# A product-based recommender on one core: fields of the last two batch tiles handled one by one, GpSimd given fewer pairs, and three matmul groups held back

## What is computed

```python
embed = tables[jnp.arange(FIELD_NUM)[None, :], sparse_inputs]     # 2048 x 26 x 32
p     = jnp.einsum('bfe,bge->bfg', embed, embed)                  # every pair of fields: a dot product of 32
l_z   = jnp.einsum('bfe,feh->bh', embed, w_z)                     # 26*32 -> 256
l_p   = jnp.einsum('bfg,fgh->bh', p, w_p)                         # pairs -> 256
l_1   = relu(concatenate([l_z + l_p + l_b, dense_inputs]))
h     = relu(l_1 @ W1 + b1)                                       # 269 -> 128
return sigmoid(h @ Wf + bf)
```

## Time and profile before

| | |
|---|---|
| profiled execution, whole | 547.92 us |
| its span (first to last instruction) | 546.1 us |
| VectorE busy | 419.9 us, 77% of the span |
| GpSimd busy | 405.7 us, 74%, of which 393.2 us in 416 gathers of 945 ns |
| TensorE busy, matmuls | 154.1 us, 28%; mean granted clock 0.616 of full speed |
| ScalarE busy | 81.2 us, 15% |

### The profile page before, as it was taken

One profiled execution on the slowest core, in us unless ns is written; L12 is line 12 of the kernel. 1 busy time (PEld: TensorE's weight loads), 2 busy tenths in 40 slices (PEclk: granted clock), 3 DMA queues, 4 the chain that ended last, 5 costly groups with the idle time before them and its releaser, 6 DMA issues.

```text
span 546.1 us, 1770 instructions
## 1 busy us (share of the span) xinstructions
PE 154.1 (28%) x244; PEld 63.2 (12%) x244; DVE 419.9 (77%) x272; ACT 81.2 (15%) x213; POOL 405.7 (74%) x430
## 2 busy tenths in 40 slices
PE   0020202402233026122117005340223633155344
PEld 0000000100011001000002001110001221033222
DVE  4204099899992459999997409899999999939993
ACT  0000000000060011100034001100006310322234
POOL 6777777777777777777777777777777777777791
PEclk9996556555657567656557556855665955566556
DMA  6263435352214434324313443434232342233320
GB/s 152 18 52 24 41 32 46 38 45 21 52 13 51 33 32 52 52 26 40 52 13 25 43 47 34 37 47 52 14 51 14 42 61 35 30 41 45 42 36 4
DMA packets 44571, 21.63 MB, mean 40 GB/s; under 512 B 24448, under 2 KB 42253, under 8 KB 44557
## 3 DMA queue, kind: packets, MB, share of 16 engines
q0 software_dynamic: 13312, 6.84, 24.5%
q1 hardware_dynamic: 31246, 14.67, 10.0%
HBM read 15.14 MB, written 6.30 MB: 39 GB/s over the span
## 4 chain that ended last, share of the span: by engine, by line
POOL 67%; issue 23%; DVE 6%; DMA 1%; PE 1%; ACT 1%; DVEq 0%; POOLq 0%; ACTq 0%
POOL rows L335 67%; DVE prod L401 3%; DVE pairs L415 2%; DMA rows<-in_L_rec_tables,which 1%; PE ps_h L665 1%; ACT pair_rows L559 1%; PE ps_h L693 0%; DMA raw<-in_r_sparse_inputs 0%; DVE rows_T L434 0%; ACT scores L597 0%; PE ps_end L701 0%; ACT hidden L590 0%; DVE pairs_T L446 0%; ACT ps_copy L538 0%; DVE wrap L374 0%
## 5 line engine op out<-in xcount | busy, mean ns | idle before, releaser
L335 POOL DMA_INDIRECT rows<-in_L_rec_tables,which x416 | 393.2, 945 | 128.3 <-issue 125.6
L401 DVE TENSOR_TENSOR prod<-ps_copy,rows 128x256 f32<-128x256 f32 (+34 forms) x130 | 197.5, 1565 | 107.8 <-ACT ps_copy L538 107.6
L415 DVE TENSOR_REDUCE pairs<-prod 128x104 f32<-128x3328 f32 (+24 forms) x58 | 191.4, 3305 | 0.0
L649 PE MATMUL ps_h<-field_rows,wz 128*128 128x512 f32 (+1 forms) x120 | 81.5, 832 | 246.5 <-DMA field_rows<-passage 246.5
L538 ACT COPY ps_copy<-rows 128x256 f32<-128x256 f32 (+3 forms) x52 | 19.6, 376 | 375.4 <-DMA rows<-in_L_rec_tables,which 375.2
L649 PEld LDWEIGHTS ps_h<-field_rows,wz 128*128 128x128 f32 x120 | 32.6, 298 | 294.8 <-DMA field_rows<-passage 241.2
L665 PE MATMUL ps_h<-pair_rows,w_pair 96*128 96x512 f32 (+5 forms) x80 | 43.7, 718 | 52.3 <-ACT pair_rows L559 52.3
L559 ACT COPY pair_rows<-pairs_T 32x384 f32<-32x384 f32 (+2 forms) x84 | 31.2, 372 | 68.4 <-DVE pairs_T L446 67.5
L693 PE MATMUL ps_h<-hidden,w 128*128 128x512 f32 (+1 forms) x20 | 13.6, 827 | 67.5 <-ACT hidden L583 67.5
L665 PEld LDWEIGHTS ps_h<-pair_rows,w_pair 96*128 96x128 f32 (+2 forms) x80 | 21.7, 282 | 76.5 <-ACT pair_rows L559 45.2
L434 DVE STREAM_TRANSPOSE rows_T<-rows 128x512 f32<-128x512 f32 (+2 forms) x35 | 19.6, 561 | 0.0
(11 more groups left out here) (24 smaller groups left out, 23.2 us busy)
## 6 DMA issues: line engine op xcount, KB each, us to landing
rows<-in_L_rec_tables,which POOLq DMA_INDIRECT x416, 3.5
passage<-rows_T SPq DMA_DIRECT2D x72, 64.0 KB, 2.6
field_rows<-passage SPq DMA_DIRECT2D x18, 256.0 KB, 4.0
passage<-rows_T SPq DMA_DIRECT2D x48, 32.0 KB, 2.2
field_rows<-passage SPq DMA_DIRECT2D x12, 128.0 KB, 2.6
wz<-in_L_rec_w_z SPq DMA_DIRECT2D x1, 768.0 KB, 5.6
w_pair<-in_w_low SPq DMA_DIRECT2D x1, 288.0 KB, 5.3
w_back<-in_w_high SPq DMA_DIRECT2D x1, 288.0 KB, 5.6
```

Source lines behind the costliest of these rows:

```text
L335: nc.gpsimd.indirect_dma_start(rows_of(p)[:, f, k, :], None, table_rows, bass.IndirectOffsetOnAxis(ap=which[:, t, f:f + 1], axis=0),).then ...
L401: ins = nc.vector.tensor_tensor(products(p, s)[:, :, at:at + high - low, :], own.broadcast_to([P, tiles, high - low, E]), rows_of(p)[:, lo ...
L415: nc.vector.tensor_reduce(pairs[:, 0:tiles_of(p), first:end], products(p, s), AX.X, ALU.add).then_inc(summed, 1)
L649: ins = nc.tensor.matmul(across(r, ps_h0[:, h, :]), wz[:, j, h * P:(h + 1) * P], side_by_side(r, field_rows[:, j, :, :, :]), start=(j == 0 ...
```

## The change

The change alters tables and one loop; no arithmetic is added or left out.

1. `ENDING` becomes 0-3, 4-7 and then fields 8 to 25 one by one. It is the list both of the units (what is copied, and what a `landed` semaphore covers) and of the stages (what is multiplied, then reduced, together). The last phase goes from 12 units and stages to 20.
2. GpSimd's share becomes 13 pairs of field 24 and 17 of field 25, 30 in place of 40. VectorE's becomes 12 and 9, 21 in place of 11.
3. Chunk 5 of the rows is turned before field 23 is multiplied, not before field 22.
4. TensorE runs, in the last phase, chunks 0 to 2, the dense part, blocks 0 and 1; then waits until field 23 has been multiplied; then chunks 3, 4, 5, block 2, the tail.

```diff
-ENDING = [(0, 4), (4, 8), (8, 12)] + [(f, f + 2) for f in range(12, 22, 2)] + [(f, f + 1) for f in range(22, 26)]
+ENDING = [(0, 4), (4, 8)] + [(f, f + 1) for f in range(8, 26)]
...
-    CHUNK_5_BEFORE = 22
-    POOL_24 = 18
-    POOL_25 = 22
+    HELD = 3
+    CHUNK_5_BEFORE = 23
+    POOL_24 = 13
+    POOL_25 = 17
...
-            for r in range(ROUNDS):
+            for r in range(END):
                 for j in range(MOVED):
                     sum_lz(r, j)
                     if j == MOVED - BLOCKS:
                         sum_dense(r)
-                    if r == END and j >= MOVED - BLOCKS:
-                        sum_lp(r, j - (MOVED - BLOCKS))
-                if r < END:
-                    for c in range(BLOCKS):
-                        sum_lp(r, c)
-                sum_lp(r, TAIL)
+                for c in range(TAIL + 1):
+                    sum_lp(r, c)
                 sum_h1(r)
                 sum_logit(r)
+
+            for j in range(HELD):
+                sum_lz(END, j)
+            sum_dense(END)
+            for c in range(BLOCKS - 1):
+                sum_lp(END, c)
+            pe.wait_ge(multiplied, STAGES_BEFORE[END] + stage_of(END, NF - LAST - 1) + 1)
+            for j in range(HELD, MOVED):
+                sum_lz(END, j)
+            for c in range(BLOCKS - 1, TAIL + 1):
+                sum_lp(END, c)
+            sum_h1(END)
+            sum_logit(END)
```

## The result

The changed kernel takes 544.68 us (median of 6 runs, 543.76 to 545.03), the kernel before 547.79 (6 runs, 546.9 to 548.23). The ratio is 0.9942, 95% interval 0.9931 to 0.9953: 3.1 us faster. The forecast was 542.7 with a range of 541.7 to 545.3, so the time lies in the range, but 2 us above the likeliest case and close to the first rival, the cold tail (544.1): it is in the range by a case that was held less likely than the forecast. The profiled execution took 543.76 us with a span of 542.0, the fastest of the six.

What follows compares the result with a forecast made beforehand. GpSimd's gathers bound the kernel to 523.1 us, then VectorE until block 2 is turned, then a ScalarE and TensorE chain. Ending at 540.75, not 546.1, saves 5.4: 547.92 to 542.5, plus 0.2 for hand-overs, 542.7; range 541.7 to 545.3.

Steps and rivals of the forecast that it cites:

- the cold tail: TensorE's clock at half, or falling in the 1.2 us gap: tail matmuls end at 536.7, time 544.1; chance 0.20.
- The bound: GpSimd's gathers, to 523.1 us, keep number and order; only what comes out of step with them can move.
- Single fields: VectorE, last phase: 5.2 us moves into its 7.59 us wait; block 2 turned at 529.7, 4.0 us earlier.
- the walk: Field-by-field count of VectorE's waits: about 0.5 at field 12, 0.7, 0.6, 0.2 and 0.2 later, 2.2 us in all.
- GpSimd's share: GpSimd's sums end at 533.3, 2.0 us earlier, after 0.8 us waiting for field 25; VectorE's tail part ends at 532.8.
- Chunk 5: Turned at about 523.8, it reaches TensorE through the DRAM buffer 6.0 us later, 529.8; nothing waits for it before block 2.
- part 4: TensorE, last phase: block 1, then chunks 3, 4, 5 without a gap from 524.6, 7.8 to 8.3 us at half clock.
- The held chunks and the clock: TensorE's clock rises to 1.00 after 4 to 6 us busy; backlog ends near 531.5, tail's four matmuls take 1.1 us.
- The sum: Tail turned 533.4, laid 534.75, warm matmuls to 535.9, end 540.75: 5.4 us less, 0.2 added, 542.7; chance 0.58.
- The lead is smaller: Landing takes 4.8 us and each added reduction 0.11: block 2 at 531.3; 543.8 warm, 545.2 cold; chance 0.14.
- Slower: ScalarE's copies of fields 9 to 17 queue behind other work, undoing VectorE's lead: 549.3; lead undone 0.08, slower 0.03.
- The hold does nothing: TensorE's wait for field 23 decides little, the order does the same work; no other time, no chance given.

Runs made afterwards that it cites:

- second profile: Changed kernel unaltered, timed once more beside the kernel before: 544.90 us, ratio 0.9944.
- fillers: Changed kernel plus two matmuls of 256 columns ahead of chunk 5's, on data already there, changing no result: 544.02 us, ratio 0.9938 to the kernel before.
- the kernel with fillers and the better share: Changed kernel plus two extra matmuls ahead of chunk 5's, GpSimd taking 17 pairs of field 24 and 11 of field 25: 542.46 us, ratio 0.9912.
- the share 17 and 11: Changed kernel with GpSimd taking 17 pairs of field 24 and 11 of field 25, no extra matmuls: 543.85 us, ratio 0.9931 to the kernel before.

## Why the prediction came out as it did, step by step

- **The bound (right).** The gathers kept their place and number; the gain came from behind them (GpSimd's pairs began at 522.96 us, beside 523.12 before).
- **Single fields (right).** Predicted: 5.2 us moved into the wait, 1.2 lost in new waits, 0.4 for 8 reductions, block 2 turned (with its 0.38) at 529.7. Measured: 529.24 in one profile of the changed kernel, 529.56 in the other. The waits shown were 1.53 us at field 11 and 0.77 at field 14, where the walk had about 1.0 at field 11 and 2.2 spread over five fields behind it: more in one place and less in the others, since landings do not come at even distances: the copies of fields 11 to 16 begin 1.5 to 2.8 us apart (ScalarE, 491.52 to 502.78), their gathers 2.5. The extra reductions cost next to nothing: a reduction of 704 elements takes 0.76 us start to start (493.00 to 493.76), 1.08 ns an element beside 1.06 for one of 1664 before. The cost per instruction that the Trainium skill states (VectorE: DVE Perf Modes, TRN2 errata), about 150 cycles or 0.16 us, was the wrong one to add here: the 0.76 us of this reduction and the 1.76 of that of 1664 elements leave 0.03 us for the fixed part, and 0.05 was enough. That following the fields one by one is needed beyond field 11 is shown by the kernel with singles for 8 to 11 alone.
- **GpSimd's share (right).** Predicted end 533.3 with 0.8 us of waiting for field 25; measured 533.40 with 0.88. VectorE's part predicted 532.8, measured 532.25, so its wait was 1.24 us and not half a us. That this step is needed for the other is shown from both sides (0.9994 and 1.0007 alone, 0.9986 with the old share).
- **Chunk 5 (wrong).** The way through the DRAM buffer was put at 6.0 us, so 529.8; it took 7.9 us (523.30 to 531.17). I had one row for this way and no bound for it. "Nothing waits for it before block 2" left out that the busy stretch of part 4 needs it: chunks 3 and 4 were done at 529.22, and block 2, laid at 532.31, stood behind it until 533.0. The two parts of the delay are in the sync queue's rows: four writes issued in 2.89 us in place of 1.73, and the read issued 3.6 us behind the last write's start, against 1.7 before. In the other profiles these four writes took 1.73 to 2.74 us to issue, and the way from turning to TensorE 6.0 to 8.3 us where a row shows it; why is open.
- **The held chunks and the clock (wrong; this is the step that cost the 2 us).** The forecast had TensorE busy without a gap from 524.6 until 531.5 (532.7 if all at half clock), the clock up in it and still up for the tail. Instead the stretch came in two parts, 5.86 us and 5.71 us busy, both at 0.50, with chunk 5's 1.95 us between them, and the tail's matmuls took 2.0 us. By the prediction's own last test ("if the tail's four matmuls take 1.9 us") this part is wrong. The price is in the profiles: the tail's matmuls were to end at 535.9 and ended at 537.0, 1.1 us; where the layers behind them are cold too (second profile) the end is at 543.0 against 540.75 in the sum, 2.2 us. Two parts of the claim were tested apart: in both profiles with fillers the clock rises and stays, and with chunk 5 earlier it rises and falls again. So the clock can be had for the tail, and the hold alone doesn't do it dependably. That the gap before chunk 5 is the reason is argued and not shown: with gaps of 1.54 and 1.31 us there, two other profiles ran chunk 5 at full clock. The rule quoted from the Trainium skill, that the moment is "run-variable", was the better guide than my count of busy us: two profiles of the same kernel differ.
- **The sum.** With block 2 and tail as forecast and a cold TensorE, the rival gave 544.1; measured 544.68. The forecast's 542.7 is what the kernel with fillers and the better share reached (542.46), with the tail turned at 533.44 and all behind it warm; that kernel has another share, so this bears out the prices and not the forecast.
- **The rivals.** *Cold tail* is what happened; its chance of 0.20, beside 0.58, was too small. That the range held the result is owed to its upper part, which stood for this rival and the next. *The lead is smaller* did not happen. *Slower* did not: VectorE's timeline has no wait at fields 16 and 17, where block 0 is laid between the copies. *The hold does nothing* fits the changed kernel (0.9934 without it), though not for the reason given: that kernel has the old order too.

## What to carry to other kernels

Where two paths end nearly level, shortening either alone gives little (here nothing that could be measured), and a test of one part alone will call it useless; look at what ends next before judging a part. Work that is pulled ahead of a wait stays ahead only if the units behind it are as fine as the arrivals, otherwise the next units take the lead back. The clock of a short tail couldn't be told from a sum of busy us here: look for every arrival that can break the busy stretch, take more than one profile of the kernel, and price the tail at the slow level unless profiles show the other.

## What the runs showed that was not expected

The kernel with fillers and the share 17 and 11 is steadier as well as faster: 542.43 to 542.81 us over five runs, where the changed kernel spreads over 1.3 and 1.8 us in its two sets of six. Neither part does that alone: with the fillers the five runs spread over 1.3 us, with the share the six spread over 2.1. Why is open. And the gathers' end itself moves between executions of kernels that are alike up to there: GpSimd's first pair multiply, which follows the last gather at once, began at 522.93 to 524.28 us in the profiles. That is 1.3 us, nearly half of the change's effect, so a single profile's end says less than the distance from this point to the end: 23.0 us before, 19.0 and 20.1 in the two profiles of the changed kernel, 17.4 in the best one.
